# Later mask merges, two of them beside the projection, and router logits inside the norm, in a graph and transformer kernel on one core

## The reference, cut to what matters

```
edge_index = jnp.stack([src, dst])
x = x + _L0_gnn_ref(_layernorm(x), ..., src, dst)
x = x + _L0_ffn_ref(_layernorm(x)[None], ...)[0]
x = x + _L1_gnn_ref(_layernorm(x), edge_index, edge_type_3, ...)
x = x + _L1_ffn_ref(_layernorm(x)[None], ...)[0]

# inside _L0_ffn_ref
logits = flat @ router_w.T                  # 1250 x 8
probs = jax.nn.softmax(logits, axis=-1)
top_w, top_i = jax.lax.top_k(probs, 2)
```

## Time and profile before

| | us |
|---|---|
| median of 3 runs | 3490.26 (3484.83 to 3490.93) |
| the profiled execution's own time | 3494.58 |
| its span, first to last instruction | 3492.8 |
| TensorE busy (products) | 2803.9 (80%) |
| VectorE busy | 2087.4 (60%) |
| ScalarE busy | 1289.4 (37%) |
| GpSimd busy | 313.8 (9%) |

### The profile page before, as it was taken

How to read it: one execution, slowest core, us unless ns; L and a number is a source line. 1 busy time by engine, 2 the same in 40 slices (tenths; PEclk the granted TensorE clock), 3 DMA queues, 4 the chain that set the end, 5 groups by cost and what they waited for, 6 DMA issues and landing times. The chain is left out here.

```text
span 3492.8 us, 36157 instructions
## 1 busy us (share of the span) xinstructions
PE 2803.9 (80%) x12912; PEld 2116.2 (61%) x12913; DVE 2087.4 (60%) x3230; ACT 1289.4 (37%) x1718; POOL 313.8 (9%) x148
## 2 busy tenths in 40 slices
PE   7654793888845984997699997895999779998869
PEld 3433793233344983554699997895788645565554
DVE  6434698999943544891688894801676863114351
ACT  2343222988710001112588882212555610003210
POOL 0000000000025853000000000510000000000002
PEclk9876755999956995998899995997999879999959
DMA  2343643411006545533523221526332511000021
GB/s 73 89 117 93 174 150 118 170 44 45 15 28 188 194 140 161 201 106 118 142 79 100 78 79 53 193 91 173 118 91 91 166 39 55 27 27 1 1 80 45
DMA packets 166538, 344.98 MB, mean 99 GB/s; under 512 B 27602, under 2 KB 92344, under 8 KB 164872
## 3 DMA queue, kind: packets, MB, share of 16 engines
q1 hardware_dynamic: 120532, 236.69, 22.2%
q10 hardware_dynamic: 36892, 90.84, 8.0%
q0 software_dynamic: 8960, 15.41, 1.7%
HBM read 259.93 MB, written 82.91 MB: 98 GB/s over the span
## 5 line engine op out<-in xcount | busy, mean ns | idle before, releaser
L1184 PE MATMUL rg1a_acc<-rg1a_values,rg1a_high 125*125 125x193 f32 x2400 | 410.7, 335 | 65.6 <-DMA rg1a_values<-values_dram 40.5
L1184 PEld LDWEIGHTS rg1a_acc<-rg1a_values,rg1a_high 125*125 125x125 f32 x2400 | 405.6, 193 | 70.8 <-DMA rg1a_values<-values_dram 43.4
L1357 PE MATMUL gat_acc<-far_u,gat_ft 125*65 125x512 f32 x720 | 289.6, 545 | 74.7 <-DVE far_u L1421 74.3
L1233 DVE TENSOR_TENSOR rg1a_high<-rg1a_high,rg1a_lowb 125x625 f32<-125x625 f32 x240 | 194.3, 810 | 149.6 <-ACT rg1a_lowb L1209 132.3
L1357 PEld LDWEIGHTS gat_acc<-far_u,gat_ft 125*65 125x65 f32 x720 | 95.5, 144 | 265.0 <-issue 173.4
L1846 PE MATMUL rg2a_acc<-rg2a_value_part,rg2a_wts_part 125*125 125x512 f32 x600 | 208.2, 347 | 50.6 <-DVE rg2a_wts_part L1611 41.1
L980 PE MATMUL rg_out<-rg_w,rg_hT 128*125 128x384 f32 x720 | 233.9, 488 | 0.0
L1208 ACT ACTIVATE rg1a_high<-rg1a_rows,rg_ks 125x625 f32<-125x625 f32 x240 | 196.5, 819 | 86.8 <-PE rg1a_acc L1184 64.1
L342 PE MATMUL sums<-src_hot,key_hot 125*125 125x512 bf16 (+1 forms) x618 | 147.9, 376 | 94.6 <-DVE key_hot L286 92.7
L1847 PE MATMUL rg2a_acc<-rg2a_value_part,rg2a_wts_part 125*125 125x512 f32 x600 | 208.4, 347 | 0.0
L1848 PE MATMUL rg2a_acc<-rg2a_value_part,rg2a_wts_part 125*125 125x512 f32 x600 | 206.7, 344 | 0.0
(11 more groups left out here) (432 smaller groups left out, 5389.5 us busy)
## 6 DMA issues: line engine op xcount, KB each, us to landing
rg2a_values<-values_dram SPq DMA_DIRECT2D x90, 384.0 KB, 3.1
rg1a_values<-values_dram SPq DMA_DIRECT2D x240, 96.0 KB, 1.9
rg_mask<-far_dram SPq DMA_DIRECT2D x60, 312.5 KB, 3.3
moe_raw<-in_L_ffn_w SPq DMA_DIRECT2D x16, 1152.0 KB, 8.1
gat_rows<-rows_dram SPq DMA_DIRECT2D x12, 1250.0 KB, 6.0
rg1a_rows<-rows_dram SPq DMA_DIRECT2D x24, 625.0 KB, 7.1
relw_chunk<-in_L_gnn_W ACTq DMA_DIRECT2D x36, 384.0 KB, 3.2
sorted_dram<-gat_zeros SPq DMA_DIRECT2D x30, 384.0 KB, 11.0
```

Of the source, the lines that this page charges most:

```text
L1184: last = pe.matmul(tile_of(u, d), wts[i % HB][:, d * TP:(d + 1) * TP], stream[i % 4][:, :], start=first and d % per_bank == 0, stop=final, ...
L1233: dve.tensor_tensor(high[i % HB][:, 0:w], high[i % HB][:, 0:w], lowb[i % LB][:, 0:w], op=ALU.max).then_inc(max_done, 1)
L1357: last = pe.matmul(acc[h % 2][0:WIDTH, b, 0:c1 - c0], ft[:, t, h, :], wts[i % HB][:, c0:c1], start=(t == 0), stop=(t == NT - 1))
```

## The change

Three edits go together.

1. In the counting loop the merge of group n moves from behind key tile 3n + 5 to behind key tile 3n + 7. Eight of the ten groups (MERGED) are merged there. Their loads stay where they were. SP also waits at the end for the stores of `far`.
2. Groups 8 and 9 are loaded and merged in `project_gat`, ahead of the ten count tiles, in the same three buffers.
3. `normalize` takes a second worker (`beside`). In the expert layer this is `RouterLogits`: it loads the router weights and expert 0's raw weights, turns the router weights, and makes the logits with the weights as the stationary operand (eight columns) and 417 tokens at a time as the moving one, in three groups, each behind the transposes of the token tile after the one it needs. ScalarE copies the three rows of logits out of PSUM, and TensorE turns them back in ten small transposes. In `route` the high parts of expert 0's weights are made by ScalarE, the low parts by GpSimd, which clears `zeros` afterwards.

```diff
+MERGED = NT - 2
@@ count_edges, SP
-                if k % 3 == 1 and k > 1:
+                if k % 3 == 1 and 0 <= k // 3 - 1 < MERGED:
                     load_masks(k // 3 - 1)
             send_counts(KT // 3 - 1)
-            load_masks(KT // 3 - 1)
             sp.wait_ge(x_in, 48)
+            for i in range(2):
+                sp.wait_ge(far_out[i], KT // 2 * 32)
@@ count_edges, VectorE
-                if k % 3 == 2 and k > 2:
-                    merge(k // 3 - 1)
-            merge(KT // 3 - 1)
-            dve.wait_ge(merged, KT // 3)
+                if k % 3 == 1 and k >= 7:
+                    merge(k // 3 - 2)
+            dve.wait_ge(merged, MERGED)
@@ normalize
+        other = beside(s) if beside else None
...
+            if other:
+                other.sync(sp)
...
             link(last)
+            if other:
+                other.vector(dve)
             link(dve.tensor_scalar(var[:, :], mean_var[:, :, 1], eps, None, op0=ALU.add))
...
+                if other:
+                    other.scalar(act)
                 act.wait_ge(copied, 2 * NT)
...
+                if other:
+                    other.turn_weights(pe)
                 for t in range(NT):
...
                     turn_tile(pe, g, banks[t % 2], dst, t, turned)
+                    if other and t >= 1:
+                        other.tensor(pe, t - 1, copied)
+                if other:
+                    other.tensor(pe, NT - 1, copied)
+                    other.finish(pe)
@@ project_gat, SP
+            for i in range(MORE):
+                n = MERGED + i
+                for a, b in SPLIT:
+                    sp.dma_start(counts[i][a:b, :].bitcast(BF16).rearrange("d (r s) -> d r s", r=R),
+                                 g.far_dram[(n * TP + a) * R:(n * TP + b) * R, :].rearrange("(d r) s -> d r s", r=R)
+                                 ).then_inc(counts_in[i], 16)
             for t in range(NT):
-                if t >= 3:
+                i = MORE + t
+                if i >= 3:
+                    sp.wait_ge(merged, min(MORE, i - 2))
+                if i >= 3 + MORE:
                     sp.wait_ge(summed, t - 2)
@@ project_gat, VectorE
+            for i in range(MORE):
...
+                dve.wait_ge(counts_in[i], 32)
+                link(dve.tensor_tensor(g.far_u[:, n, :], mask[:, 0, :], mask[:, 1, :], op=ALU.min))
+                dve.tensor_tensor(g.far_u[:, n, :], g.far_u[:, n, :], mask[:, 2, :], op=ALU.min).then_inc(merged, 1)
             for t in range(NT):
+                i = MORE + t
...
@@ new
+class RouterLogits:
+    def sync(self, sp):
+        sp.dma_start(self.rw[:, :], self.router_w).then_inc(self.w_in, 16)
+        for n in range(2):
+            self.expert_weights.load(sp, n, 0, self.first_in)
+    def vector(self, dve):
+        dve.wait_ge(self.w_turned, 1)
+        dve.tensor_copy(self.rwT[:, :, :].rearrange("p c e -> p (c e)"),
+                        self.logit_ps[:, 0:KC * self.X]).then_inc(self.w_copied, 1)
...
+    def tensor(self, pe, t, copied):
+        for k, (a, b) in enumerate(TOKENS):
+            if t != (b - 1) // TP:
+                continue
+            if k == 0:
+                pe.wait_ge(self.w_copied, 1)
+            pe.wait_ge(copied, 2 * (t + 1))
+            for c in range(KC):
+                last = pe.matmul(self.row_ps[:, k, 0:b - a], self.rwT[:, c, :], self.hT[:, c, a:b],
+                                 start=(c == 0), stop=(c == KC - 1))
+            last.then_inc(self.rows_made, 1)
+    def scalar(self, act):
+        for k, (a, b) in enumerate(TOKENS):
+            act.wait_ge(self.rows_made, k + 1)
+            act.activation(self.rows[:, a:b], self.row_ps[:, k, 0:b - a], ACT.Copy).then_inc(self.rows_out, 1)
+    def finish(self, pe):
+        X = self.X
+        pe.wait_ge(self.rows_out, len(TOKENS))
+        for t in range(NT):
+            last = pe.transpose(self.logit_ps[0:TP, t * X:(t + 1) * X], self.rows[:, t * TP:(t + 1) * TP],
+                                self.g.ident[0:X, 0:X])
...
@@ route, GpSimd
+            pool.wait_ge(first_in, 32)
+            for n in range(2):
+                pool.wait_ge(high_done, n + 1)
+                high, low = expert_weights.parts_of(n, 0)
+                pool.tensor_tensor(low, expert_weights.raw[n][:, :], high.bitcast(F32),
+                                   op=ALU.subtract).then_inc(split, 1)
             pool.memset(expert_weights.zeros[:, :], 0.0).then_inc(zeroed, 1)
             pool.wait_ge(zeroed, 1)
-            pool.wait_ge(raw_in, 32)
-            for n in range(2):
-                expert_weights.split(pool, n, 0, high_done, n + 1, split)
@@ route, TensorE
-            for t in range(NT):
-                for c in range(KC):
-                    last = pe.matmul(logit_ps[:, t * X:(t + 1) * X], hT[:, c, t * TP:(t + 1) * TP], rwT[:, c, :],
-                                     start=(c == 0), stop=(c == KC - 1))
-            last.then_inc(made, 1)
@@ route, ScalarE
+            act.wait_ge(first_in, 32)
+            for n in range(2):
+                high, low = expert_weights.parts_of(n, 0)
+                act.activation(high, expert_weights.raw[n][:, :], ACT.Copy).then_inc(high_done, 1)
             act.wait_ge(shifted, 1)
```

More of the change, by code:

```diff
@@ L420, in turn_tile, with normalize @@
     last.then_inc(tiled, 1)
[L423 removed]
+def normalize(g, tag, src, dst, dstT, gamma=None, beta=None, eps=1e-5, beside=None, stats=None):
     with ExitStack() as ctx:
@@ L1728, in load, with parts_of @@
                      self.sources[n][e, :, :].rearrange("(c p) f -> p c f", p=128)).then_inc(loaded, 16)
+    def parts_of(self, n, e):
+        at = slice(e % 2 * self.size, (e % 2 + 1) * self.size)
+        return [x[:, at] for x in self.parts[n]]
     def split(self, pool, n, e, high_done, high_count, ready):
-        at = slice(e % 2 * self.size, (e % 2 + 1) * self.size)
-        high, low = (x[:, at] for x in self.parts[n])
+        high, low = self.parts_of(n, e)
         pool.tensor_tensor(high, self.raw[n][:, :], self.zeros[:, :], op=ALU.add).then_inc(high_done, 1)
@@ L1745, in route @@
+def route(g, logit_ps, X, gate, gateT, rank, expert_weights, first_in):
     with ExitStack() as ctx:
         s = Scope(g, ctx)
-        rw = s.sb("route_w", [X, D])
-        rwT = s.sb("route_wT", [128, KC, X])
         logits = s.sb("route_logits", [TP, NT, X])
@@ L1753, in route @@
         top = s.sb("route_top", [TP, NT])
[L1754 to L1755 removed]
         gate_ps = s.ps("route_gate", [X, 3, 512])
[L1757 removed]
         v_chain, before_done, shifted, exp_done = s.sem("route_vc"), s.sem("route_before_done"), s.sem("route_shifted"), s.sem("route_exp")
         gated, gate_turned, gate_out = s.sem("route_gated"), s.sem("route_gate_turned"), s.sem("route_gate_out")
[L1760 removed]
+        zeroed, high_done, split = (s.sem(f"route_{x}") for x in ("zeroed", "high_done", "split"))
         block = s.block()
[L1763 to L1767 removed]
         @block.gpsimd
@@ L1784, in _ @@
         def _(pe):
-            pe.wait_ge(w_in, 16)
-            for c in range(KC):
-                last = pe.transpose(turn_ps[:, c * X:(c + 1) * X], rw[:, c * 128:(c + 1) * 128], g.ident[0:X, 0:X])
-            last.then_inc(w_turned, 1)
-            pe.wait_ge(w_copied, 1)
-            for t in range(NT):
-                for c in range(KC):
-                    last = pe.matmul(logit_ps[:, t * X:(t + 1) * X], hT[:, c, t * TP:(t + 1) * TP], rwT[:, c, :],
-                                     start=(c == 0), stop=(c == KC - 1))
-            last.then_inc(made, 1)
             pe.wait_ge(gated, 1)
@@ L1803, in _ @@
             link = chain(dve, v_chain)
-            dve.wait_ge(w_turned, 1)
-            dve.tensor_copy(rwT[:, :, :].rearrange("p c e -> p (c e)"), turn_ps[:, 0:KC * X]).then_inc(w_copied, 1)
-            dve.wait_ge(made, 1)
-            link(dve.tensor_copy(logits[:, :, :].rearrange("p t e -> p (t e)"), logit_ps[:, 0:NT * X]))
+            link(dve.tensor_copy(logits[:, :, :].rearrange("p t e -> p (t e)"), logit_ps[0:TP, 0:NT * X]))
             one = logits[:, :, :].unsqueeze(3).to_broadcast([TP, NT, X, X])
@@ L2245, in moe_layer @@
                 h = si.sb("moe_h", [TP, NT, D])
-                normalize(g, "moe_ln", g.x, h, hT)
-                route(g, hT, router_w, gate, gateT, rank, expert_weights)
+                logit_ps = si.ps("moe_logits", [128, 512])
+                first_in = si.sem("moe_first_in")
+                normalize(g, "moe_ln", g.x, h, hT, beside=lambda sc: RouterLogits(
+                    sc, g, hT, router_w, logit_ps, expert_weights, first_in))
+                route(g, logit_ps, X, gate, gateT, rank, expert_weights, first_in)
                 assign_slots(g, h, rank, gate, X, slots, gates, b2, gateT, table)
```

32 lines of the change are left out of this document (26 added, 6 removed).

## The result

The changed kernel takes 3402.64 us (median of four runs, 3398.09 to 3408.64) against 3488.59 for the kernel before (four runs, 3484.83 to 3490.93). The ratio is 0.9756, with a 95% interval from 0.9737 to 0.9774. The forecast was 3403.0, in a range from 3388 to 3422. The profiled execution is the fastest of its four, 3398.09, with a span of 3396.3; the one before was above its median. The two spans therefore differ by 96.5 us where the medians differ by 86.0, and the excess of some 10 us is spread between runs, not the change.

A forecast was written before the change was run, and what follows sets the result against it. Counting stage bound by ten round trips through DRAM for masks, expert layer's router block by TensorE at low clock. 76 + 8 - 3 + 6 = 87 us off the profiled 3494.58 gives 3407.6, as median 3403; range 3388 to 3422.

The forecast's parts named there:

- Waits for `masks`: Counting loop: VectorE's waits for mask landings fall from 92.7 us to 8 to 15, all in the last three merges.
- The loop, 76 us: Counting loop: at most 86.5 us of waits to gain, less 5.8 and 5.1 that merges cost, net 76 us.
- What merges give back, 10.9 us: Counting loop: late merges cost 5.8 us behind six-slice tiles (1.15 each) and 5.1 behind four-slice tiles.
- The end of the stage, 8 us: Counting stage's end to the norm: both late merges gone, last store of counts earlier, 8 us saved (4 to 9).
- Projection, 3 us lost: Projection: two merges and their mask loads ahead of the count tiles cost 3 us, between 0.7 and 5.7.
- The logits 12.6 us earlier: Expert layer's norm: wide products at full clock, 4.3 us a group, logits read at 1017.9 instead of 1030.46.
- Cold products: Rival, router logits: eight columns of the array don't keep the clock, 12.9 us more and slower transposes, 3417 us; chance 0.10.
- The route, 19.2 us: Expert layer's route: VectorE's two-input operations wait for GpSimd's subtractions, 19.2 us against 12.8 before; 14.6 if none waited.
- All hides: Rival: late merges wait for nothing and GpSimd does not hold VectorE; 105 us gained, 3385 us; chance 0.09.
- Landings grow: Rival: with gaps gone, a mask load takes 12 us instead of 7.5; 25 us lost, 3428 us; chance 0.07.
- The wait moves along: Rival, counting loop: mask loads fall behind stores, each merge waits as long as today or longer, say 3506 us; chance 0.02.

The follow-up runs named there:

- e6: Changed kernel without the eight merges in the loop and their loads, `far_u` filled with zeros by GpSimd instead; 3405.51 us, ratio 0.9753 to the kernel before.
- e8: Changed kernel with both halves of the split of expert 0's weights moved from the route into the norm; 3388.09 us, ratio 0.9695 to the kernel before.
- e9: Changed kernel with expert 0's split moved into the norm and the loop's merges three key tiles behind their old place instead of two; 3382.15 us, ratio 0.9678.
- e4: Changed kernel with the eight loop merges one key tile behind their old place instead of two; 3438.70 us, ratio 0.9848 to the kernel before.

## Why the prediction was right

The total came out within 1 us, which is partly luck, since terms were off in both directions. By its steps:

- **Waits for `masks`: 8 to 15 us, all in the last three merges of the loop.** 9.1 us in three, two of them in the last two (3.69 and 3.49) and one of 1.96 in the merge after tile 19; the one after tile 22 has none. The size was right; one place was another.
- **The loop, 76 us.** 78.4 between the two profiles. The eight stretches fell to 40.5 us where I took 42.7: a six-slice tile there takes 5.83 and not 6.32, and three of the five four-slice tiles take 4.09 and not 4.51.
- **What merges give back, 10.9 us.** 9.7 against e6, with the parts otherwise divided. Behind six-slice tiles 1.15 was too much, four of them cost 0.52 to 0.64 and the fifth 1.73. Behind four-slice tiles I had 0.5, 2.0 and 2.6; they cost nothing, 2.9 and 2.8. The reasoning held (the late ones lose what the landing is late). What it left out is the clock, 0.77 in tiles 26 and 29, 0.79 in tile 11; tile 11 stands behind a merge that waited for nothing.
- **The end of the stage, 8 us.** 8.2. SP waited 5.0 us for the last counts; they landed some 11.5 us after the close of tile 29, against 15.6 before.
- **Projection, 3 us lost.** 3.2 between these two profiles, but 6.3 over all eleven: the term was mis-sized, and even its worst case, 5.7, lies under the mean. I had taken a point between two rates of loading, 3.4 and 4.0 us a tile. The first and the last sum of counts are 34.9 us apart in the changed kernel and 37.7 in e8, 3.9 and 4.2 us for each of nine tiles, and VectorE waited for the landing of nearly each; from 280 to 310 us of the changed kernel the DMA share is 0.97 to 1.04, at 243 to 248 GB/s. TensorE waited 0.8 to 3.7 us in all for VectorE's copies of scores in the eight profiles, and not at all in the three. So the loads are behind it, at the slow rate; why the rate differs between runs of the same stage stays open.
- **The logits 12.6 us earlier.** 13.4. The row of 384 columns at 0.857 ns a column gave 4.3 us a group; measured 4.37. *Cold products* is refuted: the clock was 1.00 in the two groups shown and in the third.
- **The route, 19.2 us.** 19.4. VectorE was held by GpSimd's subtractions, as the one meeting in the earlier trace rows suggested, and e8 shows it by taking them away. The Trainium skill (SBUF — State Buffer, "Who interferes with whom") has two inputs from SBUF as the condition, against a GpSimd instruction that reads SBUF. Here the two-input operations were held, the reductions weren't, and the fill of `moe_zeros` held nobody; the trace agrees.
- **The rivals.** *All hides* was wrong for the change. e9 comes close to its number, 3382 against 3385, but not by its terms: the loop gives 85.0 for its 86 through one more tile of distance, the expert layer 16.0 for its 11 by moving the split, and the projection loses 6.5 where it had 1. By these stages and the tail's 8.0 the gain is 102.5 us of its 105; the medians give 113.5, and the rest of that is not explained by the stages. *Landings grow* would have added 22 us in the loop; 9.1 us of waits in all speak against it. *The wait moves along* fails by the same 9.1 us.

So 78.4 + 8.2 - 3.2 + 7.3 = 90.7 us stand in the touched stages of these two profiles, against 87 predicted. The medians give 86.0. With the projection at 6.3 the sum is 87.6. That the total is met to a microsecond is closer than the stages' own spread, 4.7 us in the projection alone.

## What to carry to other kernels

When a consumer waits for a round trip through DRAM, look for the distance in the loop at which the wait is gone, and go one step past where it is merely small: two tiles later left 9 us of waits, which cost 7 us of time, three tiles later left none, and the merges themselves became nearly free. Where the engine that feeds TensorE had little lead, its waits cost their whole length (e4), and the work behind them also ran at a lower clock. Before work is given to GpSimd beside VectorE, look which of VectorE's operations there take two inputs from SBUF, and move one of the two if another stage has GpSimd idle.

## What the runs showed of the hardware that was not expected

**A short gap can halve the clock, or not.** In the changed kernel TensorE stood idle 1.11 or 1.12 us before the first six products behind three different merges (tiles 8, 11 and 14):

```profile
106.87 1.40 PE L343 MATMUL sums<-src_hot,key_hot 125*125 125x512 bf16 x6 [1.12 <-DVE key_hot L288]
...
125.46 2.30 PE L343 MATMUL sums<-src_hot,key_hot 125*125 125x512 bf16 x6 [1.11 <-DVE key_hot L288]
...
145.17 1.41 PE L343 MATMUL sums<-src_hot,key_hot 125*125 125x512 bf16 x6 [1.11 <-DVE key_hot L288]
```

Twice the products took 1.4 us, once 2.30. The stretches around the second case show that the clock was at full before and soon after:

```profile
121.00:125.00 4.00, 2.96 (x18) 1.75 (x16) 3.07 (x7) 2.79 (x5) 0.00 (x0) 1.00 0.25 77
125.40:129.00 3.60, 3.54 (x13) 2.74 (x14) 1.96 (x7) 0.81 (x2) 0.00 (x0) 0.53 0.94 250
129.00:131.91 2.91, 2.53 (x15) 1.51 (x14) 1.96 (x7) 2.06 (x3) 0.00 (x0) 1.00 0.02 4
```

Equal gaps had unequal clocks, so the price of a gap of this length is a range: tile 11 cost 1.73 us, tiles 8 and 14 cost 0.58 and 0.64. What decides between them was not tested.

**A GpSimd instruction that only writes held a VectorE one with a single input.** In e6 the fill of `far_u` held the conversion from int32 to f32 for 8 us (9.92 against 1.82), although by the profile the fill began 1.1 us after the conversion (6.34 against 5.25), while in e8 the fill of `moe_zeros` held no comparison. The two differ in VectorE's operation (a conversion, against operations with two inputs) and in the fill's type and length, bf16 for 8.42 us against f32 for 2.01; which of them decides stays open.
